# A graph layer's tile list: six tiles of two node blocks and five of one at its end, in place of eight of two and one of one

## The reference

```
x = x + L0_gnn(layernorm(x), edge_weight1, src, dst)   # mean of weighted neighbours, linear
x = x + L0_ffn(layernorm(x))                           # 8 experts, top 2, hidden 512, relu
x = x + L1_gnn(layernorm(x), edge_weight, src, dst)
x = x + L1_ffn(layernorm(x))                           # 8 experts, top 2, hidden 256, gelu

L1_gnn: h = relu(x @ Wp.T + bp)                        # 128 features
        agg = sqrt(segment_sum(edge_vals * (h**2)[src], dst))
        h @ W1.T + b1 + agg @ W2.T + b2
L1_ffn: probs = softmax(x @ router.T); the two largest, rescaled to sum 1, are the weights
        x + sum over e of weight[:, e] * (gelu(x @ w1[e] + b1[e]) @ w2[e] + b2[e])
```

## Time and profile before

| | |
|---|---|
| median of three runs | 2748.9 us |
| profiled execution | 2746.08 us, its span 2744.2 us |
| TensorE busy over the span | 2265.4 us (83%) |
| VectorE | 1857.9 us (68%) |
| GpSimd | 1710.3 us (62%) |
| ScalarE | 1296.2 us (47%) |
| mean granted clock of TensorE | 0.941 |

### The profile page before, as it was taken

How to read it: one execution, slowest core, us unless ns; L and a number is a source line. 1 busy time by engine, 2 the same in 40 slices (tenths; PEclk the granted TensorE clock), 3 DMA queues, 4 the chain that set the end, 5 groups by cost and what they waited for, 6 DMA issues and landing times.

```text
span 2744.2 us, 45870 instructions
## 1 busy us (share of the span) xinstructions
PE 2265.4 (83%) x16513; PEld 1420.9 (52%) x16513; DVE 1857.9 (68%) x4929; ACT 1296.2 (47%) x2221; POOL 1710.3 (62%) x1678
## 2 busy tenths in 40 slices
PE   0137999999999999999999734588878778988987
PEld 0124555555555555555558634444444444567876
DVE  8576777778778777787776644355555555667775
ACT  4023455454454554544556601244334444566667
POOL 3677666575575665764430077777777777777760
PEclk9999999999999999999999955699999999999999
DMA  5733333343333333432220032122222222222220
GB/s 208 253 104 110 102 107 103 97 120 88 98 111 92 106 103 97 118 93 82 72 64 21 32 108 62 51 63 70 69 57 63 70 70 63 63 67 71 71 61 11
DMA packets 116317, 237.92 MB, mean 87 GB/s; under 512 B 30434, under 2 KB 70364, under 8 KB 115572
## 3 DMA queue, kind: packets, MB, share of 16 engines
q0 software_dynamic: 66560, 163.68, 21.3%
q1 hardware_dynamic: 49524, 71.26, 7.7%
HBM read 209.16 MB, written 25.67 MB: 86 GB/s over the span
## 4 chain that ended last, share of the span: by engine, by line
PE 47%; POOL 24%; DVE 12%; issue 11%; ACT 4%; DMA 2%; DVEq 0%; POOLq 0%; ACTq 0%; SPq 0%
POOL ring L625 23%; PE psY L757 18%; PE psH L721 17%; PE psM L821 4%; PE psE L703 2%; DVE hsc L1334 1%; PE psE L711 1%; DVE hid L1328 1%; DMA ring<-table,src_s 1%; PE psM L773 1%; PE psE L731 1%; PE psE L705 1%; PE psM L781 1%; ACT L1506 1%; DVE wbuf L1074 1%
## 5 line engine op out<-in xcount | busy, mean ns | idle before, releaser
L625 POOL DMA_INDIRECT ring<-table,src_s x1664 | 1680.7, 1010 | 902.4 <-issue 624.1
L721 PE MATMUL psH<-xnT,wbuf 128*128 128x512 f16 (+2 forms) x4320 | 909.9, 348 | 8.3 <-ACT hid L1517 8.3
L757 PE MATMUL psY<-hsc,wbuf 128*128 128x512 f16 (+2 forms) x4320 | 902.9, 345 | 11.2 <-DVE hsc L1334 6.2
L1517 ACT ACTIVATE hid<-psH,b,scl 128x512 f32<-128x512 f32 (+2 forms) x720 | 503.4, 699 | 761.1 <-PE psH L721 757.8
L1328 DVE TENSOR_TENSOR hid<-hid,cS 128x512 f32<-128x512 f32 (+2 forms) x720 | 427.7, 594 | 452.0 <-ACT cS L1524 310.1
L757 PEld LDWEIGHTS psY<-hsc,wbuf 128*128 128x128 f16 x4320 | 415.5, 99 | 391.4 <-issue 23.6
L721 PEld LDWEIGHTS psH<-xnT,wbuf 128*128 128x128 f16 x4320 | 406.1, 102 | 300.8 <-issue 21.1
L1334 DVE TENSOR_TENSOR hsc<-hid,hsc 128x512 f16<-128x512 f32 (+2 forms) x720 | 423.1, 588 | 0.4 <-ACT hsc L1531 0.3
L711 PE MATMUL psE<-ohbuf,ring 128*128 128x40 f32 x1664 | 251.1, 306 | 186.7 <-DMA ring<-table,src_s 186.5
L1531 ACT ACTIVATE hsc<-hid 128x512 f16<-128x512 f32 (+2 forms) x720 | 392.0, 544 | 27.1 <-DVE hid L1328 26.1
L711 PEld LDWEIGHTS psE<-ohbuf,ring 128*128 128x128 f32 x1664 | 238.3, 219 | 233.4 <-DMA ring<-table,src_s 227.9
(11 more groups left out here) (163 smaller groups left out, 1938.6 us busy)
## 6 DMA issues: line engine op xcount, KB each, us to landing
ring<-table,src_s POOLq DMA_INDIRECT x1664, 2.5
wbuf<-w_in SPq DMA_DIRECT2D x2, 4096.0 KB, 20.7
wbuf<-x_in SPq DMA_DIRECT2D x7, 896.0 KB, 12.7
table<-ring SPq DMA_DIRECT2D x7, 896.0 KB, 3.6
feat<-table SPq DMA_DIRECT2D x11, 512.0 KB, 4.0
xin<-x_in SPq DMA_DIRECT2D x11, 512.0 KB, 3.9
x_d<-x SPq DMA_DIRECT2D x11, 512.0 KB, 3.5
wbuf<-w_in SPq DMA_DIRECT2D x2, 2048.0 KB, 11.2
```

The costliest lines, as they stand in the source:

```text
L625: pool.indirect_dma_start(out=l.ring[:, g % l.R, k, :], out_offset=None, in_=l.table, in_offset=bass.IndirectOffsetOnAxis(ap=src_s[:, c:c ...
L721: last = mm(psH[n % 2][:, 0:l.TT[t]], l.w1(e, i, k, c), x[:, j, k, 0:l.TT[t]], start=(k == 0 and m == 0), stop=(k == KD - 1 and m == 2))
L757: last = mm(psY[d][:, 0:l.TT[t]], l.w2(e, i, c, d), h[:, j, 0:l.TT[t]], start=False, stop=(n == l.M - 1 and m == 2))
L1517: f(hid[(l.M * t + n) % HB][:, 0:l.TT[t]], psH[n % 2][:, 0:l.TT[t]], (ACT.Relu, ACT.Gelu)[l.i], scale=l.un_up, bias=l.b1[:, n // l.HC, n % ...
```

## The change

```diff
-ENDS = (([], [2, 2, 1]), ([], [2] * 8 + [1]))
+ENDS = (([], [2, 2, 1]), ([], [2] * 6 + [1] * 5))
```

## The result

The changed kernel takes 2785.03 us (median of four runs, 2779.66 to 2786.62), the kernel before beside it 2747.28. The ratio is 1.0137, 95% interval 1.0116 to 1.0159: 37.7 us, where 30 were forecast. The profiled execution took 2786.62 us, its span 2784.8; against the profiled execution of before that is 40.5 us.

What follows compares the result with a forecast made beforehand. Gathers were taken to bind until the last part of tile 13, compute after. Tiles 12 to 15's 144.8 us become 36.4 + 36.1 + 102.5 = 175.0, +30.2 us: 2779 by the median, range 2761 to 2796.

Steps and rivals of the forecast that it cites:

- What binds: Second layer: gathers bind only in tile 13's last part; from 2659.9 us on nothing waits for them, compute sets the end.
- Tiles 12 and 13: Four edge groups fewer in each, and narrower preparation in tile 13: 40.4 becomes 36.4 us, 38.9 becomes 36.1.
- The bare one-block tile: One-block tile preparing another, without groups: 12.6 us to the logits, 9.4 to the weights' copy, 3.0 to the next, 25.0.
- The groups: Edge groups summed in tiles 14 to 16: 0.25 us each, mostly in time where TensorE waits anyway.
- rival (b): TensorE's clock falls in one-block tiles: heavy form +10 us a tile, 2806; light form +1.5 each, inside the range; chance 0.09.
- The sum: Tiles 12 to 15's 144.8 us become 175.0 for tiles 12 to 17, 102.5 of it in 14 to 17: +30.2.
- The signs: Trace marks: gathers end near 2664, one-block tiles 24 to 27 us, weights' wait 3 or longer; wrong if clock under 0.8.
- (a): ScalarE's floor alone paces the one-block tiles, chains overlapping the steps: 21 us a tile, +12, 2761 us; chance 0.12.
- (c): Smaller tiles shorten the tail after the last landing: 16.7 us a tile, -5.5, 2743 us; chance 0.04.
- (d): Shorter tail with less overlap: one-block tiles of 17.5 to 19 us, time within 0.2% (5.5 us); chance 0.03.
- break-even of 18.1: Time per one-block tile, tiles 14 to 17, from which down the change pays: (144.8 - 72.5) / 4 us.
- The drain: About 1.38 us added to each ScalarE table load by the skill's rule, floor near 29 us a tile; the prediction rejected it.

Runs made afterwards that it cites:

- e6_early: The changed kernel with its four one-block tiles moved ahead of the six two-block tiles, 19 tiles as before; 2784.97 us, ratio 1.0137.
- e5_merged: The kernel before with one more four-block tile in place of two two-block tiles, 16 tiles; 2755.0 us, ratio 1.0029.
- e9_hold: The changed kernel with added matmuls, read by nothing, at all three places where TensorE idled over 1 us in a one-block tile; 2774.66 us, ratio 1.0109.
- e10_tables_hold: The changed kernel without table loads in preparing tiles 14 to 18, plus 24 added matmuls ahead of the weights' wait; 2746.36 us, ratio 1.0003.
- e2_tables: The changed kernel with plain copies for ScalarE's roots and exp in tiles 14 to 18, so without their six table loads each; ratio 1.0014.
- e8_before_busy: The kernel before with 32 matmuls, read by nothing, ahead of TensorE's wait for the mixing weights in preparing tiles 9 to 16; 2741.62 us, ratio 0.9982.
- e1_busy: The changed kernel with 32 matmuls, read by nothing, ahead of TensorE's wait for the mixing weights in preparing tiles 14 to 18; ratio 1.0094.

## Why the prediction was right, and which terms were off

- **What binds.** Right. The last gather starts at 2665.5 us (2663.6 before), and from there to the end it is 119.3 us instead of 80.6. e6_early and e5_merged show both bounds: one-block tiles cost the same in either place, and a tile less gains nothing.
- **Tiles 12 and 13.** Forecast 36.4 and 36.1, measured 35.9 and 34.3. A group taken out of tile 12 gave 1.1 us, close to TensorE's 1.0; tile 13 gave more than I allowed for the narrower preparation.
- **The bare one-block tile.** Forecast 25.0, as 12.6, 9.4 and 3.0 in its three stages. In the changed kernel tile 17 takes 26.7, as 13.5, 9.5 and 3.7; with the clock held 25.0, as 13.5, 9.4 and 2.1. That this last figure meets the forecast is luck: my 3.0 had a slow stretch in it, and two misses of 0.9 us cancel.
- **The groups.** I gave them 0.25 us each, hidden in TensorE's waits. They cost 0.56, 5.6 us for ten instead of 2.5.
- **The clock.** This is the mis-sized term. I had a part of one slow stretch in the last stage and called the rest rival (b). It cost 8.3 us over four tiles, 2.1 a tile, at a mean clock of 0.78 to 0.89: more than the 1.5 us a tile of (b)'s light form and far from the 10 of its heavy one. The Trainium skill ("TensorE: Matmul & The Clock Gate", Part 1) has the clock follow how busy TensorE has been of late; e9_hold agrees, with 2.4 GHz throughout once the idle places were filled.
- **The sum.** Forecast 102.5 for tiles 14 to 17, measured 113.9: 8.3 from the clock and 3.1 from the groups make the 11.4. Tiles 12 and 13 gave 2.3 back. The forecast of the whole, 2779 in 2761 to 2796, held; the medians came out 37.7 us apart instead of 30.2.
- **The signs.** Met: the gathers' end, tiles 12 and 13, twelve more table loads (139 instead of 127 in the whole trace), the last tile at 12.4. Not met: of the four tiles only the last lies in the 24 to 27 us that I gave (tile 15, at 30.5, is outside even the range of 21.5 to 30), and TensorE waits 2.0, 2.1, 2.8 and 2.8 us for the mixing weights instead of 3 or longer. The mean clock from 2650 us on is 0.85, above the 0.8 that was to show the forecast wrong, with tile 15 at 0.78.
- **The rivals.** (a): ScalarE's busy time came out at 21.1 to 21.4, but tiles took 5.6 to 9.3 us more, so it is no bound by itself. Yet the loads weigh more than my picture had it: taken away they give 6.3 to 6.7 us of tile 17, 4.5 of them ahead of the logits, where I had added 1.2 for them to what nothing hid. I had laid the middle stage to VectorE's serial chain; there two loads are worth 1.9 us and the choice of the best two 1.6. (c) and (d): even with loads gone and the clock held, tile 17 takes 18.7 us, still over the break-even of 18.1. That e10_tables_hold is level with the kernel before comes from tile 13, which prepares without loads too: tiles 12 to 17 take 65.3 + 83.6 = 148.9 us there, 4 more than the 144.8 of before. With those 65.3 the break-even is (144.8 - 65.3) / 4 = 19.9, and the four tiles take 20.9 on average.
- **The drain.** The Trainium skill ("ScalarE: Activation LUTs", What ACT_TABLE_LOAD costs) would have made six loads cost 16 us a tile, an estimate from its figures for the load and the drain. Taking them away gave 6.3 to 6.7 us in tile 17 and 7.3 at most (tile 15 of e2_tables, where the clock differs too); the measurement decides.

## What to carry to other kernels

A tile's fixed work (function table loads, a normalization, a choice of experts) doesn't shrink with its width. Before cutting tiles finer at the end of a stream, add up one engine's work that stays: here ScalarE's 20.4 us, six loads of 1.28 among them, put a floor under a tile that was above the break-even of 18.1. With the clock held and no groups to sum, a tile of two blocks took 30.4 us (tile 15 of e8_before_busy) and one of one block 25.0 (tile 17 of e9_hold): half the columns saved 5.4 us. No run here shows a finer tail that pays; behind 2660 us compute and not the landings set the end, and more tiles only added to it. And matmuls that nothing reads, put where TensorE waits anyway, kept its clock up: they shortened tiles 14 to 17 of the changed kernel by 8.3 us and tile 15 of the kernel before by 1.7. For the whole times that is 2774.66 us, 31.2 over the kernel before beside it, where the changed kernel was 37.7 over its own; the two intervals of the ratio (1.0092 to 1.0126 and 1.0116 to 1.0159) just overlap.

## What the runs showed of the hardware that was not expected

TensorE idled for over 1 us three or four times in each of tiles 15 to 17, never for more than 2.8 us, and yet its granted clock was at the lower level for 22 to 44% of the time in tiles 14 to 17 (means of 0.89 to 0.78). With 32 matmuls of 128 columns, 1.95 us, ahead of one wait, tiles 8 to 12 and 15 of the kernel before ran at 1.00 instead of 0.92 to 0.96 (e8_before_busy; its tile 13, with waits for landings, at 0.92). Of the one-block tiles only tile 17 ran at 1.00 with them (e1_busy); with matmuls at three places all four did (e9_hold). How the stretches fall on a tile changes between runs: tile 17 of the same instructions took 26.7 us in one kernel and 28.2 in another (0.88 and 0.75).

And on one chip the kernel before took 13% longer (3109 against 2747 us). In e1_busy's trace the second layer's gathers took 1277 us there, from 1732.2 to 3009.0, against the changed kernel's 1089, though a single gather took no longer (a median of 944 ns in both). 47 of them waited 109.9 us in all for something that the profile has no record of, and 43 waited 97.0 us for a ring slot. What it was, and whether the gathers or TensorE met it first, stays open.
